# Step one of a top-p attention kernel: two maxima behind each dependent operation, and the exponentials in half rows

## What is computed

```
def _top_p_attention(X, W1, W2, W3):
    q = X @ W1.T @ W2.T
    k = X @ W3.T
    probs = softmax(q @ k.T)                     # TAU = 1
    idx = argsort(-probs); sp = sorted probs; cs = cumsum(sp)
    keep those with cs - sp < 0.9                # TOP_P
    A = probs * mask
    return A / max(A.sum(-1), 1e-12)

R = S + eye(N); R = R / R.sum(-1)
for n in range(2):
    A = _top_p_attention(Xa, W1, W2, W3)
    Xf = R @ Xf
    Xa = A @ Xa
    Z = Z + Xf @ U1[n].T + Xa @ U2[n].T
h = X + Z
x = layernorm(x + layernorm(h) * ln_g + ln_b)
```

## Time and profile before

| | us |
|---|---|
| median of 3 runs | 1696.57 (1696.27 to 1696.94) |
| the profiled execution | 1698.36 |
| its span, first to last instruction | 1696.6 |
| PE, DVE, ACT, POOL busy | 1238.1, 1430.1, 872.8, 181.2 |

### The profile page before, as it was taken

The page is one execution under the profiler, slowest core; times in us unless marked ns, Lnnn a source line. Parts: engine busy times, 40 slices in busy tenths (PEclk is TensorE's granted clock), DMA queues, the critical chain, the costliest instruction groups (busy, mean ns, idle before and its releaser), DMA issues.

```text
span 1696.6 us, 29271 instructions
## 1 busy us (share of the span) xinstructions
PE 1238.1 (73%) x9162; PEld 1054.2 (62%) x9162; DVE 1430.1 (84%) x7301; ACT 872.8 (51%) x1629; POOL 181.2 (11%) x357
## 2 busy tenths in 40 slices
PE   6889887888799909796978957747754729095740
PEld 3756675667597808786867756646644628085740
DVE  3688878888856889997989988989998989899867
ACT  2677667766747525555555543524542525254320
POOL 0110010000001402212212100000000000000000
PEclk8999999999999959898989988969886959597975
DMA  5100000000022401322315130403030302112101
GB/s 172 42 1 1 2 2 1 2 1 2 2 82 82 171 32 41 122 87 77 122 41 163 41 122 1 162 1 122 1 121 2 122 1 82 41 41 82 42 0 40
DMA packets 16556, 96.40 MB, mean 57 GB/s; under 512 B 1219, under 2 KB 8898, under 8 KB 9698
## 3 DMA queue, kind: packets, MB, share of 16 engines
q1 hardware_dynamic: 16352, 94.14, 15.9%
HBM read 92.43 MB, written 1.70 MB: 55 GB/s over the span
## 4 chain that ended last, share of the span: by engine, by line
DVE 59%; PE 25%; issue 7%; ACT 5%; SPq 2%; DVEq 1%; DMA 0%; ACTq 0%; POOLq 0%; POOL 0%
DVE junkC L738 14%; DVE cand L695 14%; PE bank L516 13%; DVE E L1066 6%; PE bank L495 5%; DVE E L1068 5%; PE bank L480 5%; ACT E L586 2%; DVE slots L793 2%; DVE sub L894 2%; DVE junkS L738 2%; DVE st L746 1%; DVE st L747 1%; DVE st L748 1%; PE bank L531 1%
## 5 line engine op out<-in xcount | busy, mean ns | idle before, releaser
L613 ACT ACTIVATE blkT<-bank 128x512 f32<-128x512 f32 (+1 forms) x728 | 413.1, 568 | 529.6 <-PE bank L495 525.8
L695 DVE MAX8 cand<-E 128x8 f32<-128x32 f32 (+1 forms) x3172 | 409.5, 187 | 43.6 <-ACT E L576 43.0
L495 PE MATMUL bank<-ident,E 128*128 128x128 f32 x1144 | 194.8, 298 | 324.6 <-DVE E L1068 324.6
L516 PEld LDWEIGHTS bank<-X,blkT 128*128 128x128 f32 x2704 | 335.5, 195 | 128.7 <-issue 62.6
L516 PE MATMUL bank<-X,blkT 128*128 128x128 f32 (+1 forms) x2704 | 379.2, 284 | 44.2 <-ACT blkT L613 43.2
L495 PEld LDWEIGHTS bank<-ident,E 128*128 128x128 f32 x1144 | 152.2, 156 | 329.9 <-DVE E L1068 328.0
L738 DVE SCALAR_TENSOR_TENSOR junkC<-cand,st 128x208 f32<-128x208 f32 (+1 forms) x416 | 302.0, 762 | 3.7
L495 PE MATMUL bank<-ident,S 128*128 128x128 f32 x1560 | 240.7, 274 | 10.5 <-DVE S L1068 7.6
L480 PE MATMUL bank<-kT,Q 64*128 64x512 f32 (+1 forms) x728 | 197.3, 619 | 0.0
L495 PEld LDWEIGHTS bank<-ident,S 128*128 128x128 f32 x1560 | 185.4, 142 | 14.8 <-DVE S L1068 8.1
L516 PE MATMUL bank<-YA,blkT 128*128 128x128 f32 x1352 | 191.3, 286 | 0.0
(11 more groups left out here) (201 smaller groups left out, 1123.0 us busy)
## 6 DMA issues: line engine op xcount, KB each, us to landing
S<-in_adj_dram SPq DMA_DIRECT2D x50, 1663.5 KB, 7.1
S<-in_adj_dram SPq DMA_DIRECT2D x2, 1455.6 KB, 8.2
out_dram<-H SPq DMA_DIRECT2D x1, 1600.0 KB
X<-in_x_dram SPq DMA_DIRECT2D x6, 256.0 KB, 4.7
S<-in_adj_dram SPq DMA_DIRECT2D x2, 194.9 KB, 9.5
u_in<-in_L_gnn_U_dram SPq DMA_DIRECT2D x4, 64.0 KB, 10.3
w_in<-in_L_gnn_W_dram SPq DMA_DIRECT2D x2, 32.0 KB, 2.2
X<-in_x_dram SPq DMA_DIRECT2D x1, 64.0 KB
```

Source lines behind the costliest of these rows:

```text
L495: m = pe.transpose(BLK[early][slot][:, b * P:(b + 1) * P], src[:, j * P:(j + 1) * P], ident[:, :])
L516: m = pe.matmul(bank[int(u.acc)][:, 0:width], blkT[:, slot, b * P:(b + 1) * P], rhs[:, j, 0:width], start=(j == 0), stop=(j == NT - 1))
L613: act.activation(blkT[:, slot, 0:w], BLK[early][slot][:, 0:w], ACT.Copy).then_inc(blk_done, 1)
L695: v.max(cand[:, par, xx, 8 * r:8 * r + 8], E[where_e[self.s, self.p]][:, xx, r * w:min((r + 1) * w, N)]).then_inc(s_max, 1)
```

## The change

It touches step one only.
- `Chain` gets a fill of 2: two maxima of the next pair behind each dependent operation of the search, until the 52 are used up; behind the rest stands nothing. The reduction of the maxima (`close`) follows the last maximum at once, in the midst of the search.
- The exponentials of a pair come in five pieces: both tiles' candidates (0), and four half rows (1 to 4). Body p runs pieces 0 to 3 of pair p + 2 behind its steps 8, 9, 11 and 13, in its second half, and piece 4 of pair p + 1 at its head. Body 0 still does all of pair 1 at its head, and pair 0 stays where it was.
- The search adds the two partial sums first (L775 of the kernel after), one more dependent operation; it stood only in step two so far.

```
-    b.exps[NCH + 3] = [(0, 0, 0)]
+    b.exps[NCH + 3] = [(0, 0, k) for k in range(5)]
...
-        if p + 1 < NPAIR:
-            b.first_exps = [(0, p + 1, 0)]
+            for i, k in ((NCH + 1, 0), (NCH + 2, 1), (NCH + 4, 2), (NCH + 6, 3)):
+                b.exps[i] = [(0, p + 2, k)]
+        if p == 0:
+            b.first_exps = [(0, 1, k) for k in range(5)]
+        elif p + 1 < NPAIR:
+            b.first_exps = [(0, p + 1, 4)]
...
-                if s == 0:
-                    for xx in range(2):
+
+                n = 1 if s == 0 else 2
+                if piece < n:
+                    for xx in ((0, 1) if s == 0 else (piece,)):
                         exp_candidates(gp, s, xx)
-                        ins = exp_rows(gp, e, xx, 0, N, 0)
-                    ins.then_inc(e_ready, 1)
-                elif piece < 2:
-                    exp_candidates(gp, s, piece)
                 else:
-                    xx, half = divmod(piece - 2, 2)
+                    xx, half = divmod(piece - n, 2)
                     ins = exp_rows(gp, e, xx, half * HALF[0], HALF[0] if half == 0 else N, half)
-                    if piece == 5:
+                    if piece == n + 3:
                         ins.then_inc(e_ready, 1)
...
                         self.n += 1
+                        if self.n == self.total:
+                            self.close()
 
                 def finish(self):
                     self.step(self.total - self.n)
+
+                def close(self):
                     par = (self.s * NPAIR + self.p) % 2
                     dve.wait_ge(s_max, self.total)
...
-                if s:
-                    link(v.tensor_tensor(two(Z), Zh[:, par, :, 0], Zh[:, par, :, 1], ALU.add))
-                    z = two(Z)
-                else:
-                    z = Zh[:, par, :, 0]
+                link(v.tensor_tensor(two(Z), Zh[:, par, :, 0], Zh[:, par, :, 1], ALU.add))
+                z = two(Z)
...
-                    search(Chain(s_search, runs, 1 if s == 0 or p == 0 else 0), s, par)
+                    search(Chain(s_search, runs, 2 if s == 0 else 1 if p == 0 else 0), s, par)
```

## The result

The changed kernel takes 1701.4 us (median of 7 runs, 1699.3 to 1703.3); the kernel before, run beside it, 1696.6. The ratio is 1.0028, 95% interval 1.0016 to 1.0040: slower by 4.8 us, where 7.5 were forecast. The profiled execution has a span of 1700.0 against 1696.6, +3.4 us. That small sum hides large parts of either sign, several of which I had wrong.

What follows compares the result with a forecast made beforehand. Two coupled loops, DVE's and that of ACT and PE, bound the kernel, none full. Searches +33.0, waits -32.6, chunks +1.5, jumps +4.6 and body 12's clock +1.0 gave +7.5 us on 1696.57, so 1704 us, range 1694 to 1716.

Steps and rivals of the forecast that it cites:

- DVE pays 2.7 us a search, +33.0: Step one's searches: the second maximum costs 0.20 us, so a search takes 24.8 us; all thirteen add 33.0.
- rival (b): Second maximum costs less than 0.20 us; at 0.07 a search takes 21.4 and the kernel 1688 us. Chance 0.08.
- The waits of 32.6 us go, and 1.5 come back: DVE's step-one waits for exponentials and maxima, 32.6 us, vanish; waits for later logits chunks return 1.5.
- DVE alone sets the end, at 32.5 and 34.8; PE and ACT at 31: Step-one pair period: DVE's loop 32.5 us with a short jump gap, 34.8 with a long; PE/ACT's loop 31.
- Rival (c): Three half rows in the body's second half are not hidden; ACT's loop 35.4 us, kernel about 1716. Chance 0.15.
- ACT's wait for the maxima is free: T + 24: Mid-body, maxima are ready 24 us after a pair's pass starts (T); ACT asks at 23.5 earliest; cost 0.
- Pairs 10 and 12 turn long, +4.6: Gap between search and pass: one more instruction per pair turns pairs 10 and 12 slow, +4.6 us.
- The rule: DVE's jump over the fallback costs 2.3 us more when it leaves a window of two blocks of 128 instructions.
- The Trainium skill's blocks of 256: With 256-instruction blocks, a jump over 201 never leaves the window; no pair changes and the sum is 4.6 us lower.
- rival (a): Placement of step one's jumps changes nothing in sum; +2.9, 1699.5 us, no difference. Chance 0.22.
- Body 12's clock, +1.0: Body 12, following body 11, may start at PE's low clock: 0 to 2.2 us, taken as +1.0.
- Step two, +-2 us: Step two, same code at other addresses, was let stand at +-2 us.

Runs made afterwards that it cites:

- e1: The kernel before with two maxima behind each dependent operation in step one and their reduction at once, exponentials still whole rows at the body's head: 1703.5 us.
- e2: The changed kernel with a fill of 1, so exponentials in half rows but one maximum behind each dependent operation: 1698.3 us.
- e4: The changed kernel with one and two maxima in turn (fill 1.5) behind step one's dependent operations, exponential pieces where the changed kernel has them: 1679.1 us.
- e5: The changed kernel with fill 1.5, candidates behind step 10, half rows behind 11 and 13, two half rows at the next body's head: 1679.7 us.
- e10: e9 with a fill of 1.25, candidates behind step 11, half rows behind 12 and 13, two at the head: 1662.0 us.
- e3: The changed kernel with 64 waits that pass at once (32 DVE instructions) ahead of step one, moving only addresses: 1702.0 us.
- e7: The changed kernel with 36 never-executed instructions in each pair's fallback branch in step one, jumps 384 apart: 1717.0 us.
- e8: e7 with 214 waits that pass at once (107 instructions) also ahead of step one: 1683.7 us.
- e11: The kernel before with 37 jumped-over instructions in each pair's fallback and 107 waits' instructions ahead of step one: 1692.2 us.
- e9: e5 with e8's padding, 36 jumped-over instructions per pair and 107 ahead of step one: 1666.9 us.
- e12: The kernel before with 37 jumped-over instructions in each pair's fallback, without the 107 ahead of step one: 1688.5 us.

## Why the prediction was right, and where it was not

The time came out 2.6 us from the forecast, inside the range and on its side. By its own steps:

- **DVE pays 2.7 us a search, +33.0.** Held: +34.75. Operation to dependent operation 0.46 for 0.47, a search 24.8 to 25.4 behind a short gap for 24.8. The price of the second maximum was taken from the group of eight rather than from the first one, and rival (b) falls with it.
- **The waits of 32.6 us go, and 1.5 come back.** 29.1 net for 31.1. The first operation waits less than 0.5 us from pair 1 on, as said; the maxima wait 2.8 us, in pairs 1, 2, 6 and 10, a little over the 1.5. Of the reason the step was half wrong: e1 shows that the longer search alone removes them, e2 that the half rows alone don't.
- **DVE alone sets the end, at 32.5 and 34.8; PE and ACT at 31.** Periods are 32.7 to 32.9 (one 33.9) where the next gap is short, and 35.0 to 36.1 where it is long. e4 and e5 show DVE alone binding, e10 shows the other loop at 30.9. Rival (c) falls: the half rows are hidden.
- **ACT's wait for the maxima is free: T + 24.** They came at T + 24.4, and ACT waited 3.0 us in three pairs in all. With a fill of 1 it waits 49.5 (e2), so the early maxima are a condition of this.
- **Pairs 10 and 12 turn long, +4.6.** This step failed. The six long pairs stayed the six, gaps 1.29 and 1.27 in 10 and 12. The rule was right (e3, e7 and e8 hit every pair), the count that it was used with was not. With jumps 349 and 350 apart, every arc that fits the 13 gaps before makes pair 12 long after, and it stayed short. With 347 and 348 the change moves pair 10 by eleven places and pair 12 by thirteen, to where the 13 gaps before leave open whether they are long: the term had bounds of 0 and 4.6, and I gave it the upper one. The price was also short: 3.0 us in full rather than 2.3 (e7 and e8).
- **The Trainium skill's blocks of 256** (Runtime: NRT & Kernel Launch, Instruction fetch mechanics), rival (a). Its result for the six gaps came true by accident. Its size did not hold for DVE: by 256 neither e3 nor e7 would have any other gap than the changed kernel, and DVE's packets are of 8.2 KB. That a taken branch outside of what is loaded stops the engine, as the page says, is what the 74 long gaps show, each with its packet.
- **Body 12's clock, +1.0.** 1.3 measured. Ahead of it stands a term I had not: 2.0 us of late instructions while the adjacency is loaded.
- **Start of the first search**, not in the sum: +2.0, of which 0.5 is that pair 0's exponentials now come in five pieces. 1.4 is there already at ACT's first eviction (43.48, 44.90), ahead of all that was changed; the first search starts anywhere from 58.4 to 61.5 us in the kernels of the table, so this is scatter between executions.
- **Step two, +-2 us.** Mis-sized: -8.0. It has jumps like step one's, and I had the rule in hand that says that they change when the code moves. The kernels of the table go by it: where DVE's unexplained waits in step two are 61.0, 58.2, 54.9 and 50.0 us (before, e1, changed, e11), step two takes 1126.4, 1123.8, 1118.4 and 1114.9. Of the other nine, eight lie within 2 us of that line and e9 3.5 below it.

So the nearness is luck in large part. Against the profiled execution's +3.3 the forecast had 12.6 us too much (4.6 of jumps that did not come, 8.0 that step two gave back) and 8.4 too little (searches 1.8, waits 2.0, start 2.0, late read 2.0, clock 0.3, and 0.35 that is left over). The first two terms were right in kind and make a small plus, but they do not carry the sign: without the 4.6 us that failed, the forecast was +2.9, which by its own bound of 1700.0 is no difference. And the sign is not the change's alone. With long gaps everywhere the change costs 28 us (1688.5, 1717.0), with short ones it gains 8 (1692.2, 1683.7). At the places where the two kernels happened to lie it costs 5.

## What to carry to other kernels

A wait that a longer chain of work takes up is not won: before counting it, ask whether the engine's own new work would have covered it anyway, and then pay for as little of that work as brings the others' data in time (here 1.25 maxima for an operation, not 2). Where an engine's program is long and has jumps, compare two kernels at more than one placement of the code; a padding that does no work moved this one by 33 us. And an idle engine that is delayed is not always a loss: look where its low clock falls.

## What the runs showed of the hardware

- A forward jump of DVE over 201 instructions (237 or 238 in the padded kernels) leaves a gap of 1.1 to 1.6 us or of 3.3 to 3.9, and which of them is set by its place in the program, with a period of 128 instructions. In the long one a packet of 8.2 KB of instructions comes. It fits a window of two blocks of 128: a jump over 201 would then be long from 73 of the 128 places and one over 237 from 109, and the gaps leave 65 to 77 and 75 or more.
- The long gap of pair 12 is 3.6 us in e9, e11 and e12, and 6.0, 6.5 and 6.9 in e3, e7 and e8. The two windows, of e8 and of e12, are the 2.6 and 3.5 us before the pass:

```profile
474.00:476.60 2.60, 0.00 (x0) 0.00 (x0) 0.00 (x0) 0.00 (x0) 0.00 (x0) 0.57 1.01 423
```
```profile
476.00:479.50 3.50, 3.50 (x34) 3.50 (x33) 0.00 (x0) 2.19 (x6) 0.69 (x2) 1.00 0.01 2
```

  In e8 the adjacency is coming in at 423 GB/s, in e12 nothing is (2 GB/s). The packet of instructions starts 4.1, 4.6 and 5.0 us into the gap in e3, e7 and e8, where without the load it was 1.2 to 2.0, and the pass follows 1.6 us behind it as ever; in e9 the packet came 0.4 us ahead of the load's first one, and was not late. So instructions that have to be fetched came 2.4 to 3.3 us later behind this load. The late reads of 1.95 us in the changed kernel and of 1.97 in e5, at the same place, are such a fetch too (its packet 3.9 us behind the start of the pass in both): there the load was issued 1.5 and 1.0 us ahead of the pass, in e2 and e4 0.6 us behind it, in e1 and the kernel before later still, and these four have no such wait. No run moved the load alone.
- More time at the low clock is not always more time in all. Over the eleven periods e12 has a mean granted clock of 0.93 and e11 of 0.95 (e12 first below), and e12 is not the slower. Its PE also stands less, 37 us for 52 (length less busy time below), and it waits for ACT 5.5 us up to pair 12's pass where e11 waits 55.9.

```profile
84.58:450.73 366.15, 328.83 (x2166) 243.30 (x2165) 314.45 (x1563) 263.91 (x503) 23.38 (x49) 0.93 0.01 2
```
```profile
81.71:455.36 373.65, 321.29 (x2156) 247.81 (x2155) 313.96 (x1562) 263.79 (x502) 24.27 (x49) 0.95 0.01 2
```
